# Two cross-attention layers on one core: another order of the loads and of every engine, energies of both halves together, the MLP in three groups

## The chip, the cores and the metric

One core of one Trainium2 chip runs the whole program. Times are microseconds (us) on the device, from the start of the execution to its end. "Before" is the kernel as it was, "after" the changed one.

## The reference

`x` and `ctx` (called `y` in the first layer) are 16 x 64 x 256. Layer 0 works on each of the 16 batches with channels in rows:

```python
x_q = einsum('oc,bcn->bno', w_qk, y);  x_k = einsum('oc,bcn->bon', w_qk, x)
x_v = einsum('oc,bcn->bon', w_v, x) + b_v
energy = einsum('bnc,bcm->bnm', x_q, x_k)             # 256 x 256 for each batch
attention = softmax(energy);  attention /= 1e-07 + attention.sum(axis=1, keepdims=True)
x_r = einsum('bcn,bnm->bcm', x_v, attention)
x = x + relu(einsum('oc,bcn->bon', w_t, x - x_r) + b_t)
```

Layer 1 is a transformer block on 64 tokens a batch, width 256:

```python
q = layer_norm(x) @ q_w + q_b;  k = ctx @ k_w + k_b;  v = ctx @ v_w + v_b      # 16 heads of 16
hidden = softmax(where(mask, q @ k.T * 0.25, min)) @ v @ cproj_w + cproj_b + x
out = hidden + gelu(layer_norm(hidden) @ fc_w + fc_b) @ proj_w + proj_b        # inner width 1024
```

## The kernel before

Two batches share the 128 partitions, so there are eight pairs, n = 0 to 7. Index e (0 or 1) is a batch of the pair: partitions 0 to 63 or 64 to 127. All tensors stay on chip; every engine has one long list of steps written out by hand, and runs it strictly in that order, with semaphore waits between engines. All eight PSUM banks are assigned by hand.

Layer 0, for each pair: `proj(n)` multiplies the pair by `gram` (w_qk times itself, into `gx`) and by the folded value weight (into `uext`); `energy(n, e)` makes one batch's 256 x 256 energies out of `ys` and `gx` with 64 rows of the array; `energy_max` (VectorE), `energy_exp` (ScalarE), `rowsum_inv` (VectorE) and `scale_u` (GpSimd) follow for each batch; `mix(n)` multiplies; `colsum_inv`, `mix_normed`, `relu_in`, `relu`, `residual` finish the pair. `wtx(n)` is w_t times x. An fp32 matmul is two MATMUL records in the trace.

The setup before the first pair: `wt`, `wv`, `wqk` are loaded; `wt` is turned, `gram` made, the two bias rows (`vec0_rows`) turned, and `wtv`, `wtbv` made. SyncE, ScalarE and GpSimd each issue some loads. Twelve records of `ones` times `ones` run ahead of all this.

Layer 1: `turn_ctx`, `make_keys`, `make_values`, `make_queries` run for two halves of four pairs. `scores(n)`, softmax steps on VectorE, ScalarE and GpSimd (`probs_normed`), `turn_probs`, `heads`, `cproj`, `hidden`, `hidden_norm`, `turn_hidden`, `hidden_weight`, `hidden_high`, `hidden_low` follow for each pair; the last three leave the normed activations as a high and a low part (`hidT`). The MLP runs for halves of four pairs: `fc(k)`, k = 0 to 15, makes 128 of the 1024 inner rows for 512 columns (three products of high and low parts, twice: six MATMULs); `gelu(k)` and `split_ff(k)` bring them to `ff`; `project(n)` is 24 MATMULs of 256 columns over the eight blocks of a half, and `result(n)` adds the residual before the output's DMA. `fc(8)` to `fc(15)` are the second half; their columns lie in the same `ff` as the first half's, so they are written only when `project(3)` is done.

## Time and profile before

| | us |
|---|---|
| median of 3 runs (lowest, highest) | 157.91 (156.69, 158.32) |
| the profiled execution, its own time | 157.12 |
| its span in the trace | 155.3 |
| TensorE busy | 144.1 (93%) |
| VectorE busy | 110.4 (71%) |
| ScalarE busy | 97.1 (63%) |
| GpSimd busy | 92.0 (59%) |

The span goes from the first to the last instruction in the trace; 1.8 us of the execution's time lie around it. Busy is the time in which an engine had at least one instruction under way, with the pipeline's fill and drain, so that an engine that is busy all the time need not be at its fastest; the distance from one start to the next tells what an instruction really takes of TensorE.

### The profile page before, as it was taken

To read this page: it belongs to the slowest core of one execution; us is meant where nothing else is said; L and a number is where in the kernel's file an instruction comes from. 1 tells how busy PE (TensorE), PEld (TensorE's weight loads), DVE (VectorE), ACT (ScalarE), POOL (GpSimd) and SP (SyncE) were. 2 spreads that over 40 slices of the span, in tenths; PEclk is the share of its full clock that TensorE was granted. 3 is DMA by queue.
4 is the path that set the end of the run, shared out by engine and by line. 5 is a ranking of instruction groups with operands and counts; after the bars stand their busy time and mean duration, and the time that the engine had idled before them with its cause. 6 is when DMAs were issued, how large, how long until landed. Compare 5 with 4: busy or idle time off the path is not lost.

```text
span 155.3 us, 3653 instructions
## 1 busy us (share of the span) xinstructions
PE 144.1 (93%) x1284; PEld 114.3 (74%) x1284; DVE 110.4 (71%) x249; ACT 97.1 (63%) x242; POOL 92.0 (59%) x148
## 2 busy tenths in 40 slices
PE   7369999999999989969999999999999999999993
PEld 6256767867778738836757686877788999789992
DVE  2232759999998769899798996999898120788211
ACT  2101668858698995898898999896971452453000
POOL 8950541696858787558879897559799372000000
PEclk9955999999999999999999999999999999999999
DMA  1999020002200020201010000000000110001011
GB/s 26 327 294 305 23 68 0 6 2 68 70 0 4 0 68 0 74 2 54 25 61 4 4 0 0 4 2 0 4 0 4 34 36 0 0 4 68 34 51 51
DMA packets 6787, 6.89 MB, mean 44 GB/s; under 512 B 1044, under 2 KB 6194, under 8 KB 6770
## 3 DMA queue, kind: packets, MB, share of 16 engines
q1 hardware_dynamic: 5808, 5.85, 11.7%
q10 hardware_dynamic: 674, 0.56, 1.2%
q0 software_dynamic: 288, 0.27, 0.7%
q8 instruction: 10, 0.16, 0.4%
q14 instruction: 7, 0.06, 0.1%
HBM read 5.62 MB, written 1.05 MB: 43 GB/s over the span
## 4 chain that ended last, share of the span: by engine, by line
PE 52%; ACT 16%; POOL 11%; issue 7%; DVE 5%; ACTq 0%; DVEq 0%; POOLq 0%
PE psum L754 48%; POOL probs L344 4%; POOL rows L349 2%; ACT vals L413 2%; ACT probs L463 2%; ACT hdT L383 2%; DVE smax L642 2%; ACT hn L480 2%; ACT keys L383 2%; ACT ys L499 1%; POOL hid_rstd_t L291 1%; POOL hidT_lo L354 1%; PE psum L880 1%; ACT att L427 1%; POOL rows L339 1%
## 5 line engine op out<-in xcount | busy, mean ns | idle before, releaser
L344 POOL TENSOR_TENSOR probs<-probs,pinv 128x512 f32<-128x512 f32 x16 | 18.1, 1139 | 6.2 <-DVE pinv L666 6.1
L319 POOL TENSOR_SCALAR us<-uext,rinv 128x128 f32<-128x128 f32 x32 | 12.6, 406 | 15.0 <-DVE rinv L614 14.8
L427 ACT ACTIVATE att<-psum,nmax 128x256 f32<-128x256 f32 x32 | 14.8, 473 | 7.9 <-DVE nmax L608 7.9
L754 PE MATMUL psum<-wpj_hi,ff_hi 128*128 128x256 f32 x64 | 18.4, 288 | 0.0
L754 PE MATMUL psum<-wpj_lo,ff_hi 128*128 128x256 f32 x64 | 18.0, 281 | 0.0
L754 PE MATMUL psum<-wpj_hi,ff_lo 128*128 128x256 f32 x64 | 17.9, 280 | 0.0
L499 ACT ACTIVATE ys<-psum,vec 128x512 f32<-128x512 f32 x16 | 11.0, 693 | 10.0 <-PE psum L754 8.0
L704 DVE CAST ff_hi<-ys 128x512 fp32r<-128x512 f32 x16 | 9.1, 569 | 8.8 <-ACT ys L499 8.8
L754 PE MATMUL psum<-att,us 128*128 128x256 f32 x64 | 15.2, 381 | 0.0
L754 PE MATMUL psum<-gx,ys 64*128 64x256 f32 x64 | 13.7, 434 | 0.4 <-issue 0.4
L608 DVE TENSOR_REDUCE nmax<-psum 128x2 f32<-128x512 f32 x16 | 10.7, 682 | 4.6 <-PE psum L754 4.4
L706 DVE TENSOR_TENSOR ff_lo<-ys,ff_hi 128x512 fp32r<-128x512 f32 x16 | 13.4, 839 | 0.5
L754 PE MATMUL psum<-hidT_hi,wfc_hi 128*128 128x512 f32 x32 | 13.1, 409 | 0.0
L754 PEld LDWEIGHTS psum<-att,us 128*128 128x128 f32 x64 | 11.6, 190 | 1.6 <-issue 0.3
L754 PE MATMUL psum<-hidT_lo,wfc_hi 128*128 128x512 f32 x32 | 12.7, 395 | 0.0
L754 PE MATMUL psum<-hidT_hi,wfc_lo 128*128 128x512 f32 x32 | 12.6, 395 | 0.0
L754 PEld LDWEIGHTS psum<-wpj_hi,ff_hi 128*128 128x128 f32 x64 | 12.1, 188 | 0.3 <-DVE ff_lo L706 0.2
L754 PEld LDWEIGHTS psum<-wpj_lo,ff_hi 128*128 128x128 f32 x64 | 12.1, 189 | 0.0
L754 PEld LDWEIGHTS psum<-wpj_hi,ff_lo 128*128 128x128 f32 x64 | 12.1, 188 | 0.0
L754 PEld LDWEIGHTS psum<-gx,ys 64*128 64x128 f32 x64 | 8.4, 202 | 4.1 <-ACT att L427 1.7
L661 DVE TENSOR_REDUCE psums<-probs 128x8 f32<-128x512 f32 x16 | 10.5, 669 | 0.5 <-ACT probs L463 0.3
L651 DVE TENSOR_TENSOR probs<-psum,smax 128x512 f32<-128x512 f32 x16 | 10.6, 681 | 0.2
(126 smaller groups left out, 382.8 us busy)
## 6 DMA issues: line engine op xcount, KB each, us to landing
wstage<-in_L_xattn_fc_w_dram SPq DMA_DIRECT2D x4, 256.0 KB, 4.9
wstage<-in_L_xattn_proj_w_dram SPq DMA_DIRECT2D x4, 256.0 KB, 2.7
out_dram<-rows SPq DMA_DIRECT2D x8, 128.0 KB, 1.7
ys<-in_ctx_dram SPq DMA_DIRECT2D x1, 512.0 KB, 6.1
rows<-in_x_dram SPq DMA_DIRECT2D x1, 512.0 KB, 7.3
ys<-in_ctx_dram ACTq DMA_DIRECT2D x1, 384.0 KB, 6.0
rows<-in_x_dram SPq DMA_DIRECT2D x1, 384.0 KB, 6.4
wk<-in_L_xattn_k_w_dram SPq DMA_DIRECT2D x1, 256.0 KB, 6.6
```

Source lines behind the costliest of these rows:

```text
L319: pool.tensor_scalar(us[:, n % 2, e, j, :], uext[:, n % 2, j, e * C:e * C + P], rinv[:, n % 2, e, j:j + 1], 1.0, ALU.mult, ALU.mult).then_ ...
L344: pool.tensor_tensor(half, half, pinv[:, n % 2, HEAD_HALVES[i]].unsqueeze(2).broadcast_to([P, H // 2, C]), ALU.mult).then_inc(S["probs_rea ...
L349: pool.tensor_tensor(rows[:, n, :], rows[:, n, :], proj_b[:], ALU.add).then_inc(S["hid_plus_bias"], 1)
L383: act.activation(dst, src, ACT.Identity, bias=bias, scale=scale).then_inc(S[done], 1)
L427: act.activation(att[:, n % 2, e, j, :], halfbank(ENERGY + e, j), ACT.Exp, bias=nmax[:, n % 2, e, j:j + 1], accum_out=rsum[:, n % 2, e, j: ...
L499: act.activation(act_ff[:, k % 2, :], bank(FC_BANK[k]), ACT.Gelu_apprx_tanh, bias=col(FC_B + k % M)).then_inc(S["gelu_ready"], 1)
L608: dve.tensor_reduce(nmax[:, n % 2, e, :], bank(ENERGY + e).rearrange("p (j m) -> p j m", j=2), AX.X, ALU.max, negate=True).then_inc(S["ene ...
L651: dve.tensor_tensor(probs[:, n % 2, i * BANK:(i + 1) * BANK].rearrange("p (j i k) -> p j i k", j=2, k=C), scores_ps[:, 2 * i:2 * i + 2].re ...
L661: dve.tensor_reduce(psums[:, n % 2, HEAD_HALVES[i]], half, AX.X, ALU.add).then_inc(S["probs_sum"], 1)
L704: dve.tensor_copy(ff[0][:, m, :], act_ff[:, k % 2, :]).then_inc(S["ff_hi"], 1)
L706: dve.tensor_tensor(ff[1][:, m, :], act_ff[:, k % 2, :], ff[0][:, m, :].bitcast(F32), ALU.subtract).then_inc(S["ff_lo"], 1)
L754: return pe.matmul(dst, lhsT, rhs, start=start, stop=stop)
```

## The change

- **Loads.** SyncE issues `w_qk` first (it was on ScalarE), then `w_t`, `w_v`, the two rows `b_v`, `b_t` (they were on GpSimd), then pairs 1 to 3 of `x`, the key and value weights, the second half of `ctx` and `x`, and only then the eight vectors of layer 1. ScalarE issues pair 0 of `x`, then pair 0 of `ctx`. The four small mask loads go from GpSimd to SyncE behind `q_w`.
- **Setup.** TensorE makes `gram` first; `proj(0)` is cut into `make_gx(0)`, ahead of `wtv` and the turned biases, and `make_u(0)`, behind the first energies. The energies of pair 0 come ahead of `wtbv`, of the turned context and of `proj`'s second part.
- **Energies.** `energy(n)` makes both batches of a pair in one step, one instruction of e = 0, one of e = 1 in turn, and waits until all four exponentials of pair n - 1 are done. In the kernel before both halves are steps of their own; between those of pairs 1, 5 and 6 other steps stand.
- **MLP.** `GROUPS` has three groups: pairs 0 to 3 (512 columns), 4 and 5 (256), 6 and 7 (256): 24 `fc` steps in place of 16, the last 16 half as wide. Group 1 writes columns 0 and 1 of `ff`, which pairs 0 and 1 had (`pairs_before` gives 2), group 2 columns 2 and 3 (it waits for four `project`).
- **Order.** All engines' lists are written anew, and the banks with them. Some waits that another one implies are left out.

```diff
-        CTX_BANK, KEYS_BANK = [4, 7, 5, 7], [7, 6, 4, 4]
-        VALUES_BANK, QUERIES_BANK = [6, 7, 5, 4], [0, 7, 7, 5]
-        FC_BANK = [5, 1, 0, 7, 3, 0, 4, 5, 6, 4, 6, 0, 1, 5, 0, 6]
-        PROJECT_BANK = [0, 5, 3, 2, 7, 3, 1, 5]
+        GROUPS = [(0, 4, 0), (4, 2, 0), (6, 2, 2)]
+        CTX_BANK, KEYS_BANK = [4, 6, 6, 7], [7, 7, 4, 7]
+        VALUES_BANK, QUERIES_BANK = [7, 5, 4, 5], [6, 7, 4, 5]
+        FC_BANK = [1, 0, 6, 2, 3, 0, 5, 2, 3, 0, 3, 0, 2, 5, 5, 3, 6, 4, 3, 6, 0, 4, 0, 3]
+        PROJECT_BANK = [7, 5, 1, 1, 7, 6, 0, 1]
+
+        def group_of(n):
+            return next((k, g) for k, g in enumerate(GROUPS) if g[0] <= n < g[0] + g[1])
+
+        def pairs_before(k):
+
+            at, end = GROUPS[k][2], GROUPS[k][2] + GROUPS[k][1]
+            return max([f + min(n, end - a) for f, n, a in GROUPS[:k] if a < end and at < a + n], default=0)
...
         def _(sp):
+            load_twice(sp, "w_qk", wqk, wqk_loaded)
             load_twice(sp, "w_t", wt0, wt_loaded)
             load_twice(sp, "w_v", wv0, wv0_loaded)
-            load_pairs(sp, "x", rows, x_loaded, 0)
+            load_vec(sp, 0, "b_v", L0_BV, vec0_loaded)
+            load_vec(sp, 0, "b_t", L0_BT, vec0_loaded)
             load_pairs(sp, "x", rows, x_loaded, 1)
             load_weight(sp, "k_w", wk, "k")
+            load_weight(sp, "v_w", wv, "v")
+            load_pairs(sp, "ctx_2048", ys, y_loaded, 2)
+            load_pairs(sp, "x", rows, x_loaded, 2)
             for name, at in (("ln1_w", LN1_W), ("ln1_b", LN1_B), ("q_b", Q_B), ("k_b", K_B), ("v_b", V_B),
                              ("ln2_w", LN2_W), ("ln2_b", LN2_B), ("fc_b", FC_B)):
                 load_vec(sp, 1, name, at, vec_loaded)
-            load_weight(sp, "v_w", wv, "v")
-            load_pairs(sp, "ctx_2048", ys, y_loaded, 2)
-            load_pairs(sp, "x", rows, x_loaded, 2)
             load_weight(sp, "q_w", wq, "q")
+            sp.wait_ge(mask_zeroed, 1)
+            for j in range(J):
+                sp.dma_start(mask8[32 * j:32 * j + 2, :, :], A["mask_BxS2_bf1"].rearrange(
+                    "(n e) k -> e n k", e=2)).then_inc(w_loaded["mask"], 16)
             load_weight(sp, "cproj_w", wc, "c")
...
-            load_vec(pool, 0, "b_v", L0_BV, vec0_loaded)
-            load_vec(pool, 0, "b_t", L0_BT, vec0_loaded)
+            pool.memset(uext[:], 1.0).then_inc(zeros_ready, 1)
             pool.memset(half_power[:], -0.5).then_inc(zeros_ready, 1)
-            pool.memset(uext[:], 1.0).then_inc(zeros_ready, 1)
+            pool.memset(mask8[:], 0).then_inc(mask_zeroed, 1)
             pool.memset(vals[:], 0.0).then_inc(zeros_ready, 1)
-            pool.memset(mask8[:], 0).then_inc(mask_zeroed, 1)
+            pool.wait_ge(zeros_ready, 3)
             pool.wait_ge(mask_zeroed, 1)
-            for j in range(J):
-                pool.dma_start(mask8[32 * j:32 * j + 2, :, :], A["mask_BxS2_bf1"].rearrange(
-                    "(n e) k -> e n k", e=2)).then_inc(w_loaded["mask"], 16)
-            pool.wait_ge(zeros_ready, 3)
...
-            load_twice(act, "w_qk", wqk, wqk_loaded)
+            load_pairs(act, "x", rows, x_loaded, 0)
             load_pairs(act, "ctx_2048", ys, y_loaded, 0)
             load_pairs(act, "ctx_2048", ys, y_loaded, 1)
...
-                wait(act, "mixed", 2 * (n - 2) + e + 1)
+                if e == 0:
+                    wait(act, "mixed", 2 * (n - 1))
...
-                act.activation(act_ff[:, k % 2, :], bank(FC_BANK[k]), ACT.Gelu_apprx_tanh,
+                width = GROUPS[k // M][1] * P
+                act.activation(act_ff[:, k % 2, 0:width], psum[:, FC_BANK[k], 0:width], ACT.Gelu_apprx_tanh,
                                bias=col(FC_B + k % M)).then_inc(S["gelu_ready"], 1)
...
-                m = k % M
+                m, (first, count, at) = k % M, GROUPS[k // M]
+                cols, src = slice(at * P, (at + count) * P), act_ff[:, k % 2, 0:count * P]
                 wait(dve, "gelu_ready", k + 1)
 
-                wait(dve, "mlp_made", NH * (k // M))
-                dve.tensor_copy(ff[0][:, m, :], act_ff[:, k % 2, :]).then_inc(S["ff_hi"], 1)
+                if m == 0:
+                    wait(dve, "mlp_made", pairs_before(k // M))
+                dve.tensor_copy(ff[0][:, m, cols], src).then_inc(S["ff_hi"], 1)
                 wait(dve, "ff_hi", k + 1)
-                dve.tensor_tensor(ff[1][:, m, :], act_ff[:, k % 2, :], ff[0][:, m, :].bitcast(F32),
+                dve.tensor_tensor(ff[1][:, m, cols], src, ff[0][:, m, cols].bitcast(F32),
...
+            def make_gx(n):
                 if n == 0:
                     pe.wait_ge(gram_ready, 2)
+                landed(pe, x_loaded, n)
+                mm(halfbank(PROJ0, 0), gram[:], rows[:, n, :]).then_inc(S["gx_made"], 1)
+
+            def make_u(n):
+                if n == 0:
                     pe.wait_ge(wtv_ready, 2)
-                landed(pe, x_loaded, n)
-                mm(halfbank(PROJ0, 0), gram[:], rows[:, n, :])
                 for j in range(2):
                     ins = mm(psum[:, PROJ0, D + j * P:D + (j + 1) * P], rows[:, n, j * P:(j + 1) * P], wtvT[:])
-                ins.then_inc(S["proj_made"], 1)
-
-            def energy(n, e):
+                ins.then_inc(S["u_made"], 1)
+
+            def proj(n):
+                make_gx(n)
+                make_u(n)
+
+            def energy(n):
                 wait(pe, "gx_ready", n + 1)
                 landed(pe, y_loaded, n)
-                r = slice(e * C, (e + 1) * C)
                 for j in range(2):
-                    ins = mm(halfbank(ENERGY + e, j), ys[r, n, j * P:(j + 1) * P], gx[r, n % 2, :])
-                ins.then_inc(S["energy_made"], 1)
+                    for e in range(2):
+                        r = slice(e * C, (e + 1) * C)
+                        ins = mm(halfbank(ENERGY + e, j), ys[r, n, j * P:(j + 1) * P], gx[r, n % 2, :])
+                        if j == 1:
+                            ins.then_inc(S["energy_made"], 1)
...
-                h, i = k // M, k % M
-                wait(pe, "hid_lo", NH * (h + 1))
+                (first, count, _), i = GROUPS[k // M], k % M
+                wait(pe, "hid_lo", first + count)
                 if k == 0:
                     wait(pe, "part_lo", WPARTS // 2)
                 for c in range(G):
                     for a, b in ((0, 0), (0, 1), (1, 0)):
-                        ins = mm(bank(FC_BANK[k]), wfc[a][:, c, i * P:(i + 1) * P],
-                                 hidT[b][:, c, h * TOK:(h + 1) * TOK], c == 0 and a + b == 0,
+                        ins = mm(psum[:, FC_BANK[k], 0:count * P], wfc[a][:, c, i * P:(i + 1) * P],
+                                 hidT[b][:, c, first * P:(first + count) * P], c == 0 and a + b == 0,
                                  c == G - 1 and (a, b) == (1, 0))
                 ins.then_inc(S["fc_made"], 1)
 
             def project(n):
-                h, i = n // NH, n % NH
+                k, (first, count, at) = group_of(n)
+                cols = slice((at + n - first) * P, (at + n - first + 1) * P)
                 if n == 0:
                     wait(pe, "part_lo", WPARTS)
                 for m in range(M):
-                    if i == 0:
-                        wait(pe, "ff_lo", M * h + m + 1)
+                    if n == first:
+                        wait(pe, "ff_lo", M * k + m + 1)
                     for a, b in ((0, 0), (0, 1), (1, 0)):
-                        ins = mm(halfbank(PROJECT_BANK[n], 0), ff[a][:, m, i * P:(i + 1) * P], wpj[b][:, m, :],
+                        ins = mm(halfbank(PROJECT_BANK[n], 0), ff[a][:, m, cols], wpj[b][:, m, :],
...
-            proj(0); pe.wait_ge(wtbv_ready, 1); turn_ctx(0, 0); energy(0, 0); energy(0, 1)
-            wait(pe, "u_ready", 1); proj(1); turn_ctx(0, 1); wtx(0); wait(pe, "energy_exp", 2); energy(1, 0)
...
+            keep_warm(6); make_gram(); turn_wt(); make_gx(0); make_wtv(); turn_vec0(); energy(0)
+            pe.wait_ge(bv_ready, 1); make_wtbv(); wait(pe, "gx_ready", 1); make_u(0); pe.wait_ge(gram_ready, 2)
+            wtx(0); pe.wait_ge(wtbv_ready, 1); turn_ctx(0, 0); wait(pe, "u_ready", 1); proj(1)
...
+            hidden_weight(6); hidden_high(6); hidden_normed(7); gelu(12); gelu(13); gelu(14); hidden_weight(7)
...
+            split_ff(5); split_ff(6); split_ff(7); hidden(6); hidden_mean_var(6); split_ff(8); split_ff(9)
+            result(0); result(1); split_ff(10); hidden(7); hidden_mean_var(7); split_ff(11); split_ff(12)
...
+            wait(pe, "gelu_ready", 5); fc(8); wait(pe, "gelu_ready", 7); turn_probs(7, 1); fc(9)
+            wait(pe, "hidf_ready", 12); project(0); wait(pe, "hidden_ready", 7); heads(7)
             wait(pe, "probst_ready", 16); project(1); wait(pe, "heads_ready", 16); cproj(7)
...
+            turn_hidden(7); wait(pe, "gelu_ready", 14); fc(14); fc(15); wait(pe, "out_ready", 3); project(3)
+            wait(pe, "hidden_ready", 8); fc(16); fc(17); wait(pe, "gelu_ready", 16); fc(18)
```

What TensorE is given between its warm-up and the energies of pair 0, before:

```order
L754 MATMUL psum<-ones 128x128 x6
L754 MATMUL psum<-ident,wt 64x64 x2
L754 MATMUL psum<-wqk 64x64 x2
L771 MATMUL psum<-ident,vec_rows 128x2
L754 MATMUL psum<-wtT,wv 64x64 x2
L754 MATMUL psum<-wtT,bv_cols 128x128
L754 MATMUL psum<-rows,gram 128x256
L754 MATMUL psum<-wtvT,rows 128x128 x2
L827 MATMUL psum<-ident,ys 128x128 x4
L754 MATMUL psum<-gx,ys 128x256 x4
L754 MATMUL psum<-rows,gram 128x256
```

And after, from `ones` to the first energies and behind them:

```order
L777 MATMUL psum<-ones 128x128 x6
L777 MATMUL psum<-wqk 64x64 x2
L777 MATMUL psum<-ident,wt 64x64 x2
L777 MATMUL psum<-rows,gram 128x256
L777 MATMUL psum<-wtT,wv 64x64 x2
L807 MATMUL psum<-ident,vec_rows 128x2
L777 MATMUL psum<-gx,ys 128x256 x4
L777 MATMUL psum<-wtT,bv_cols 128x128
L777 MATMUL psum<-wtvT,rows 128x128 x2
L777 MATMUL psum<-rows,wtT 128x256
L868 MATMUL psum<-ident,ys 128x128 x4
```

`gram` (`psum<-wqk`) and the `gx` product (`psum<-rows,gram`) now come early, the first energies (`psum<-gx,ys`) are the seventh row and not the tenth, and the turned context (`psum<-ident,ys`) stands behind them.

TensorE around the energies of pair 5, before:

```order
L754 MATMUL psum<-att,us 128x256 x4
L754 MATMUL psum<-gx,ys 128x256 x2
L754 MATMUL psum<-rows,wtT 128x256
L754 MATMUL psum<-gx,ys 128x256 x2
L754 MATMUL psum<-rows,gram 128x256
L754 MATMUL psum<-wtvT,rows 128x128 x2
L754 MATMUL psum<-att,us 128x256 x4
```

After:

```order
L777 MATMUL psum<-att,us 128x256 x4
L777 MATMUL psum<-gx,ys 128x256 x4
L860 MATMUL psum<-ident,xn 128x128 x2
L777 MATMUL psum<-rows,gram 128x256
L777 MATMUL psum<-wtvT,rows 128x128 x2
L777 MATMUL psum<-rows,wtT 128x256
```

The two halves of `psum<-gx,ys`, x2 each with `psum<-rows,wtT` between, have become one step x4.

ScalarE in the last third, from pair 7's turned probabilities on (`ys<-psum,vec` is a GELU), before:

```order
L499 ACTIVATE ys<-psum,vec 128x512 x2
L383 ACTIVATE hidf<-psum,vec 128x128 x2
L469 COPY prT<-psum 128x512 x2
L480 ACTIVATE hn<-rows,shift,hid_rstd_t 128x256
L383 ACTIVATE hdT<-psum,vec 128x128 x2
L493 CAST hidT_hi<-hidf 128x2x128
L383 ACTIVATE hidf<-psum,vec 128x128 x2
L493 CAST hidT_hi<-hidf 128x2x128
L480 ACTIVATE hn<-rows,shift,hid_rstd_t 128x256
L383 ACTIVATE hidf<-psum,vec 128x128 x2
L493 CAST hidT_hi<-hidf 128x2x128
L499 ACTIVATE ys<-psum,vec 128x512 x8
```

After:

```order
L483 COPY prT<-psum 128x512
L513 ACTIVATE ys<-psum,vec 128x256
L393 ACTIVATE hdT<-psum,vec 128x128 x2
L494 ACTIVATE hn<-rows,shift,hid_rstd_t 128x256
L513 ACTIVATE ys<-psum,vec 128x256 x2
L393 ACTIVATE hidf<-psum,vec 128x128 x2
L506 CAST hidT_hi<-hidf 128x2x128
L494 ACTIVATE hn<-rows,shift,hid_rstd_t 128x256
L513 ACTIVATE ys<-psum,vec 128x256 x3
L393 ACTIVATE hidf<-psum,vec 128x128 x2
L506 CAST hidT_hi<-hidf 128x2x128
L513 ACTIVATE ys<-psum,vec 128x256 x9
```

The eight GELUs of 512 columns in the last row before are sixteen of 256 columns, seven of which now stand between the steps of pairs 6 and 7.

## Rows read from the trace of the kernel before

**Rows 1.** The page of the profile: span, and busy time of each engine.

```profile
span 155.3 us, 3653 instructions
...
PE 144.1 (93%) x1284; PEld 114.3 (74%) x1284; DVE 110.4 (71%) x249; ACT 97.1 (63%) x242; POOL 92.0 (59%) x148
```

**Rows 2.** Windows: length, busy us (instructions) of PE, PEld, DVE, ACT, POOL; clock, DMA share, GB/s.

```profile
21.86:46.70 24.84, 24.46 (x126) 18.55 (x126) 23.41 (x60) 19.20 (x65) 16.09 (x32) 1.00 0.07 23
46.70:98.00 51.30, 48.26 (x662) 34.91 (x665) 44.93 (x101) 45.96 (x108) 40.88 (x62) 1.00 0.07 23
98.00:152.75 54.75, 54.54 (x432) 48.18 (x424) 32.83 (x61) 26.11 (x53) 22.60 (x31) 1.00 0.05 18
```

**Rows 3.** TensorE by time, 0 to 17 us: start, duration, operation, idle before.

```profile
1.05 2.93 PE L754 MATMUL psum<-ones 128*128 128x128 f32 x12 [1.05 <-POOL ones L268]
4.03 0.48 PE L754 MATMUL psum<-ident,wt 64*64 64x64 f32 x4
5.03 0.33 PE L754 MATMUL psum<-wqk 64*64 64x64 f32 x4 [0.52 <-DMA wqk<-in_L_xattn_w_qk_dram]
7.15 0.22 PE L771 MATMUL psum<-ident,vec_rows 2*128 2x2 f32 x1 [1.79 <-DMA vec_rows<-in_L_xattn_b_t_dram]
...
8.53 0.80 PE L754 MATMUL psum<-wtT,bv_cols 128*128 128x128 f32 x2 [0.90 <-DVE bv_cols L557]
...
12.79 2.09 PE L754 MATMUL psum<-gx,ys 64*128 64x256 f32 x8
...
16.75 1.13 PE L754 MATMUL psum<-gx,ys 64*128 64x256 f32 x4
```

**Rows 4.** Issue of the first loads: SyncE's first, and ScalarE's first and next.

```profile
0.80 0.66 SPq L224 DMA_DIRECT2D wt<-in_L_xattn_w_t_dram  x1
...
0.79 1.38 ACTq L224 DMA_DIRECT2D wqk<-in_L_xattn_w_qk_dram  x1
2.21 0.85 ACTq L231 DMA_DIRECT2D ys<-in_ctx_dram  x2
```

**Rows 5.** DMA issues by tensor: count, size, us from issue to landing.

```profile
rows<-in_x_dram SPq DMA_DIRECT2D x1, 128.0 KB, 4.8
ys<-in_ctx_dram ACTq DMA_DIRECT2D x1, 128.0 KB, 4.3
...
vec_rows<-in_L_xattn_b_t_dram POOLq DMA_DIRECT2D x1, 0.5 KB, 4.9
```

**Rows 6.** TensorE and its granted clock in single microseconds of the start (windows).

```profile
8.00:9.00 1.00, 0.47 (x2) 0.50 1.08 339
14.00:15.00 1.00, 1.00 (x7) 0.59 0.85 277
```

**Rows 7.** TensorE in order of time, the energies and what follows them.

```profile
21.86 1.14 PE L754 MATMUL psum<-gx,ys 64*128 64x256 f32 x8
...
25.73 1.14 PE L754 MATMUL psum<-gx,ys 64*128 64x256 f32 x8
26.80 0.70 PE L754 MATMUL psum<-rows,wtT 128*128 128x256 f32 x2
...
34.94 1.10 PE L754 MATMUL psum<-gx,ys 64*128 64x256 f32 x4 [0.37 <-issue]
35.97 0.70 PE L754 MATMUL psum<-rows,wtT 128*128 128x256 f32 x2
```

**Rows 8.** TensorE in order of time, one `fc` and one `project`, two starts of each.

```profile
102.43 0.39 PE L754 MATMUL psum<-hidT_lo,wfc_hi 128*128 128x512 f32 x1
102.67 0.40 PE L754 MATMUL psum<-hidT_hi,wfc_lo 128*128 128x512 f32 x1
...
117.00 0.28 PE L754 MATMUL psum<-wpj_hi,ff_hi 128*128 128x256 f32 x1
117.12 0.28 PE L754 MATMUL psum<-wpj_lo,ff_hi 128*128 128x256 f32 x1
```

**Rows 9.** Costliest groups on the page: ScalarE's exponentials.

```profile
L427 ACT ACTIVATE att<-psum,nmax 128x256 f32<-128x256 f32 x32 | 14.8, 473 | 7.9 <-DVE nmax L608 7.9
```

353 lines of the change are left out of this document (178 added, 175 removed).

## Prediction

> **What bounds the kernel now.** I read the page first: TensorE is busy for 144.1 of 155.3 us, no other engine for more than 110.4 [rows 1]. That is an average, so I asked for the same by stretch. From 21.86 to 46.70 TensorE is busy 24.46 of 24.84 us, from 46.70 to 98 us 48.26 of 51.30, and from there to the last matmul 54.54 of 54.75 [rows 2]. The reader should see two things there: the whole MLP part has 0.2 us of TensorE's time to give, and what TensorE waits for lies in the middle stretch (3.0 us) and ahead of 12.79 us. VectorE (44.93 of 51.30) and ScalarE (45.96) are close behind it in the middle stretch, so TensorE is the bound, but not by much.
>
> Busy need not be useful, so the third view is TensorE's list in order of time. At the start there are holes: 0.52 us for the load of `wqk`, 1.79 us for the turned bias row, 0.90 us for `bv_cols`; the first energies start only at 12.79 us, and run at half clock (x8 takes 2.09 us; later 1.14) [rows 3, 7]. The granted clock is 0.50 from 8 us on and is back at 1 within the microsecond from 14 us (0.59 in its mean): 1.2 and 2.4 GHz [rows 6]. It fell behind the hole of 1.79 us and rose after some six microseconds of nearly unbroken work.
>
> **Part 1, the start.** What leaves the path: the wait for `wqk` behind ScalarE's slow first issue (1.38 us against 0.66 us of SyncE's first, whose data the turning of `wt` found in place at 4.03) [rows 3, 4]; the bias rows' landing as a condition for everything; and `wtbv`, the second part of `proj(0)` and the turned context, which move behind the first energies.
>
> When can `energy(0)` start? `ys` of pair 0 keeps its place on ScalarE: issued at 2.21, 4.3 us to landing, 6.5 us [rows 4, 5]. `rows` of pair 0 becomes ScalarE's first load: 0.79 plus 4.8 gives 5.6; its product with `gram` at half clock takes two records, about 0.9, and a hop through VectorE another 0.9, which is what such a hop costs at 8.53: `gx` is there at 7.4 [rows 3 to 5]. The row `b_t` is SyncE's fifth load and its turning stands ahead of the energies in TensorE's list: 0.80 plus four issues of at most 0.66 is 3.4, plus 4.3 to 4.9 gives 7.7 to 8.3 [rows 4, 5]; it has half a kilobyte, so it may well be earlier. I take 7.8, 5.0 us ahead of today's 12.79.
>
> Not all of it is kept, since the moved steps are now between `energy(0)` and `energy(1)`. Today that distance is 16.75 - 12.79 = 3.96. The stretch from 8.53 to 12.79 (4.26 us) less the `gx` product (0.9) and a wait of some 0.7 leaves 2.7 us of steps that join it, at half clock. With today's clocks `energy(1)` would come at 7.8 + 3.96 + 2.7 = 14.5. At full clock throughout it is 7.8 + (3.96 - 1.0) + 1.35 = 12.1; at half clock throughout the 1.95 us now run after 14.8 double, 16.4. The holes of 1.79 and 0.90 shrink, so an earlier rise is likelier than a later one. I take 13.8, a gain of **3.0** (bounds 0.3 and 4.6). From there on TensorE has no idle time up to 46.7 to speak of, so a shift is kept.
>
> The other moved issues: the four mask loads now stand on SyncE ahead of `cproj_w` and the MLP weights, about four times 0.3 to 0.66, one to three microseconds later for loads that are used from some 33 us on; and SyncE's wait for the mask's memset, behind which `cproj_w` and the staged weights queue, ends long before SyncE comes to it at some 8 us, since GpSimd has only two small memsets ahead. GpSimd loses six issues before 12 us, where it waits anyway. I price all this at nothing; without that cover a late MLP weight would cost its delay once, up to 2 us.
>
> **Part 2, energies of both halves together.** The list shows x8 with 1.07 us from its start to the next step (25.73 to 26.80), and x4, one half alone, with 1.03 (34.94 to 35.97) [rows 7]. So the two halves, which use different 64 rows of the array, already run beside each other where they stand next to each other, and a half alone costs as much as both. Pairs 1, 5 and 6 have separate halves today, the other five stand together (pair 7 with a few ns between). The change therefore saves 3 x 1.03 = **3.1** us of TensorE, and nothing in the other pairs; turning e = 0 and e = 1 within a step changes nothing that the rows show.
>
> A rule of the Trainium skill speaks otherwise: "TensorE: Matmul & The Clock Gate", "The mechanism", says that matmuls start and end strictly in program order, and only weight loads are pulled ahead. By that rule x8 in today's order (four records of one half, then four of the other) would take twice an x4; the trace disagrees, with 1.14 us against 1.10.
>
> What it adds is a wait: `energy(n)` needs all four exponentials of pair n - 1, where the first half needed two. Queued behind it on TensorE are `proj(n+1)`, `wtx` and `mix(n-1)`, and VectorE's maxima wait for it. From pair 2 to pair 3 the halves stood together and the distance was 25.73 - 21.86 = 3.87 us without idle time [rows 7]; the mean distance of the five pairs from 21.86 to 46.70 is 24.84 / 5 = 4.97. Less two lone halves it is 4.55, above 3.87, so the new wait should mostly be over when it is reached.
>
> **Part 3, other engines.** With three microseconds less of TensorE's time, VectorE's 23.41 us and ScalarE's 19.20 [rows 2] have to fit in some 22.5 in the first stretch. VectorE's busy time holds overlapping tails, so this is no hard bound, yet some of the 3.1 will return as waits: I take **0.8** back (0 to 3.1). In the stretch from 46.7 to 98 us the order is new and I can't price it step by step: today's waits are 3.0 us in all, so it can't give more than that, and an equal loss bounds it above. I take 0: the engines' sums stay as they are, and the list is no denser.
>
> **Part 4, the MLP.** Two starts of an `fc` of 512 columns are 0.24 us apart (102.43, 102.67), of 256 columns 0.12 (117.00, 117.12) [rows 8]. The 48 records of `fc(8)` to `fc(15)` at 0.24 become 96 at 0.12; by the mean over a longer run of them (0.233, 0.118) that is 11.2 against 11.3 us, a cost of **0.1**. The gain can't be more than the 0.2 us that TensorE is idle from 98 us on. ScalarE gets eight GELUs more and VectorE eight more splits, under a stretch in which they are busy for 26.11 and 32.83 of 54.75 [rows 2]; at up to 1 us each they still fit. The shared columns add waits: `split_ff(8)` waits for `project(1)`, and `hidden(7)` is queued behind it, behind `split_ff(10)` and two results. I count some 4 us of VectorE there, then some 3 us of norm and turning, against `fc(10)` to `fc(13)` and `project(2)` on TensorE, 48 records of 0.118 or 5.7 us, and `cproj(7)`: about level, so between 0 and 1.5 us. I take 0.
>
> **The sum.** -3.0 - 3.1 + 0.8 + 0.1 = -5.2 us. The profiled execution took 157.12, so it would be 151.9. The median of the runs is 157.91, 0.8 above it; I forecast against the median: **152.7**. A difference of 1% (1.6 us) is about what this kernel's runs can tell from none.
>
> **The rivals.**
> - *The clock stays low to the end of the start.* The half-clock bound of part 1: gain 0.3 in place of 3.0, the rest as above, -2.5, 155.4 us. For it: the clock did fall there. Against: the hole before the fall shrinks. (The same page of the Trainium skill, "What's actually happening", calls the low clock the idle default; this trace agrees, with 0.50 behind the 1.79 us hole.) 15%.
> - *ScalarE or VectorE takes over.* All of the 3.1 comes back, and the middle stretch loses as much as it waits today, 3.0: -3.0 + 3.0 + 0.1, 158.0 us. For it: 90% and 88% busy in the middle. 12%.
> - *Slower: the loop over the exponentials.* ScalarE works 19.20 / 5 = 3.84 us a pair, of which four exponentials of 0.473 are 1.9 [rows 2, 9]. If none of the other 1.9 lay in the shadow of energies and maxima, since the order puts a `norm_weight` between the two halves of pair 6, the distance would be 3.87 + 1.9 = 5.8 and not 4.97: six times 0.83 is +5.0; with the start's -3.0 and 0.9, +2.9 or 160.8 us. It is slower by 1% from a distance of 5.6 on. 5%.
> - *More than forecast.* The full-clock start (4.6), nothing given back, and two of the three microseconds of waits in the middle gone: -9.6, 148.3 us; half of the surplus gives 150.5. 9%.
> - *The interleaving itself makes the overlap*, in all eight pairs: five more times 1.03, -10.4 and 147.5 us. That is the page's rule; [rows 7] speaks against it. 2%.
> - *The forecast*, 150.8 to 154.8: 57%.
>
> **Range and chances.** From 149.6 to 156.6: it takes in the low-clock case and part of the better one. Faster by over 1%: 57 + 15 + 9 + 2 = 83%; within 1%: 12%; slower: 5%.
>
> **What would show it.** First energies at 7.8 us and the second x8 at 13.8; eight energies of x8 with 1.07 us to the next step, none of x4; a distance of 4.5 us a pair; the clock's level from 8 to 14 us; TensorE's idle time in the middle near 3 us; `fc` of 256 columns at 0.118 from start to start and an end part without idle time. I am wrong if the energies' distance stays at 5, if the start's gain is gone by pair 2, or if TensorE waits ahead of `fc(14)` to `fc(18)`.

## The result, and the profile after

| | before | after |
|---|---|---|
| median of the runs | 158.12 us (4 runs, 156.69 to 158.86) | 152.04 us (4 runs, 151.90 to 152.48) |
| ratio | | 0.963 (95%: 0.956 to 0.970) |
| the profiled execution | 157.12 us, span 155.3 | 152.17 us, span 150.4 |

Faster by 3.7%; the forecast was 152.7. A few executions of a kernel run over 1.5% longer than its fastest: here and below they count in the medians and the highest times, and not in the ratios. The page of the kernel after, span and busy time of each engine, against [rows 1]:

```profile
span 150.4 us, 3717 instructions
...
PE 140.8 (94%) x1332; PEld 114.6 (76%) x1332; DVE 116.2 (77%) x265; ACT 99.3 (66%) x250; POOL 87.2 (58%) x142
```

TensorE lost 3.3 us of busy time. VectorE shows 5.8 us more, although its work grew only by eight splits: 4 us of that is one cast in the start, shown below. Windows of after, the three stretches that answer to [rows 2] (from the x8 of pair 2 to that of pair 7, to the first `fc`, to the end):

```profile
18.72:42.76 24.04, 23.79 (x133) 18.46 (x132) 23.00 (x61) 20.31 (x67) 17.32 (x34) 1.00 0.08 26
42.76:96.00 53.24, 50.41 (x698) 36.78 (x698) 48.36 (x106) 48.28 (x114) 41.88 (x67) 1.00 0.08 22
96.00:150.40 54.40, 51.03 (x427) 47.32 (x426) 32.56 (x71) 25.39 (x54) 19.71 (x26) 1.00 0.06 21
```

TensorE's gap in the middle is 2.8 us, against 3.0 before. (In the last row 3.4 us are not busy: the row runs to the end of the span, 2.6 us past the last matmul, and holds two waits of 0.4 us each, shown under e9.) The start, TensorE in order of time, against [rows 3]:

```profile
1.05 2.93 PE L777 MATMUL psum<-ones 128*128 128x128 f32 x12 [1.05 <-POOL ones L282]
4.37 0.48 PE L777 MATMUL psum<-wqk 64*64 64x64 f32 x4 [0.39 <-DMA wqk<-in_L_xattn_w_qk_dram]
6.42 0.48 PE L777 MATMUL psum<-ident,wt 64*64 64x64 f32 x4 [1.58 <-DMA wt<-in_L_xattn_w_t_dram]
6.83 1.22 PE L777 MATMUL psum<-rows,gram 128*128 128x256 f32 x2
...
8.58 2.08 PE L777 MATMUL psum<-gx,ys 64*128 64x256 f32 x8
10.59 0.79 PE L777 MATMUL psum<-wtT,bv_cols 128*128 128x128 f32 x2
...
14.86 1.14 PE L777 MATMUL psum<-gx,ys 64*128 64x256 f32 x8
```

`energy(0)` starts at 8.58 in place of 12.79 and `energy(1)` at 14.86 in place of 16.75. The reader should see a hole that wasn't there: 1.58 us for `wt`, which had been in place at 4.03. Its half-clock length (2.08 for x8) is unchanged.

The energies further on, against [rows 7]:

```profile
31.31 1.14 PE L777 MATMUL psum<-gx,ys 64*128 64x256 f32 x8
32.37 0.44 PE L860 MATMUL psum<-ident,xn 128*128 128x128 f32 x2
...
36.43 1.13 PE L777 MATMUL psum<-gx,ys 64*128 64x256 f32 x8
37.49 0.70 PE L777 MATMUL psum<-rows,wtT 128*128 128x256 f32 x2
```

From start to next step it is 1.06 us, in pairs 5 and 6 too.

**One ruler for all runs.** Three marks on TensorE cut every trace: the start of `energy(1)`, the start of `energy(7)`, and the last record of `project(7)`. Each number is a difference of two starts in the TensorE list, in us, taken in ns and then rounded, so that it may be 0.01 off the rows; before it is 152.43 - 16.75, after 147.57 - 14.86:

| kernel | energy(1) at | to energy(7) | to the last record | both | median of runs |
|---|---|---|---|---|---|
| before | 16.75 | 29.68 | 106.00 | 135.68 | 158.1 |
| after | 14.86 | 27.90 | 104.82 | 132.72 | 152.04 |
| e1_adjacent | 17.71 | 28.85 | 105.94 | 134.79 | 156.89 |
| e2_not_turned | 14.87 | 27.93 | 104.78 | 132.71 | 151.95 |
| e3_apart | 13.92 | 31.12 | 104.25 | 135.37 | 154.46 |
| e4_old_loads | 14.74 | 27.92 | 104.77 | 132.69 | 152.95 |
| e5_old_setup | 18.87 | 27.90 | 104.81 | 132.71 | 155.67 |
| e6_two_halves | 15.65 | 27.90 | 104.44 | 132.34 | 152.23 |
| e7_warm | 12.59 | 27.90 | 104.79 | 132.70 | 150.47 |
| e8_clean_start | 12.69 | 27.90 | 104.81 | 132.71 | 150.05 |
| e9_tail | 15.26 | 27.91 | 103.96 | 131.87 | 151.59 |
| e10_all | 11.60 | 27.91 | 103.97 | 131.88 | 148.55 |
| e11_cast_late | 14.56 | 27.91 | 104.80 | 132.71 | 151.77 |
| e12_best | 13.59 | 27.90 | 104.06 | 131.96 | 148.49 |

Seven kernels that have the same work and order behind `energy(1)` (after, e2, e4, e5, e7, e8, e11) agree in "both" within 0.03 us, while their `energy(1)` is spread over six microseconds. What differs among these seven profiles is the start, and whatever is won there is kept whole. So I read each profile by the ruler. If the part behind `energy(1)` is the same in all runs of a kernel (only one run of each has a trace), a median less the "both" of its row says how a typical start goes: 22.4 us before, 19.3 after.

### The profile page after: what moved, and what is told of

It is laid out like the page before. It is cut to its first block, busy times and chain, and to the rows that moved or that the text cites. A ratio compares the mean times of both kernels' runs of the same rounds, so it can differ in the third digit from the quotient of the medians.

```text
span 150.4 us, 3717 instructions
## 1 busy us (share of the span) xinstructions
PE 140.8 (94%) x1332; PEld 114.6 (76%) x1332; DVE 116.2 (77%) x265; ACT 99.3 (66%) x250; POOL 87.2 (58%) x142
## 3 DMA queue, kind: packets, MB, share of 16 engines
HBM read 5.62 MB, written 1.05 MB: 44 GB/s over the span
## 4 chain that ended last, share of the span: by engine, by line
PE 39%; POOL 20%; issue 17%; DVE 17%; DMA 3%; ACT 2%; SPq 0%; POOLq 0%; DVEq 0%; ACTq 0%
PE psum L777 37%; POOL probs L354 5%; DMA wt<-in_L_xattn_w_t_dram 3%; POOL rows L359 2%; POOL hid_rstd_t L300 2%; DVE nmax L628 2%; POOL hidT_lo L364 2%; DVE probs L670 2%; POOL wpj_lo L321 2%; DVE xn L655 2%; ACT vals L424 1%; POOL us L329 1%; DVE mixn L640 1%; POOL shift L310 1%; PE psum L921 1%
## 5 line engine op out<-in xcount | busy, mean ns | idle before, releaser
L439 ACT ACTIVATE att<-psum,nmax 128x256 f32<-128x256 f32 x32 | 14.8, 474 | 11.6 <-DVE nmax L628 11.6
L513 ACT ACTIVATE ys<-psum,vec 128x256 f32<-128x256 f32 (+1 forms) x24 | 12.9, 545 | 14.3 <-PE psum L777 10.9
L725 DVE CAST ff_hi<-ys 128x256 fp32r<-128x256 f32 (+1 forms) x24 | 10.0, 415 | 12.7 <-ACT ys L513 8.6
L329 POOL TENSOR_SCALAR us<-uext,rinv 128x128 f32<-128x128 f32 x32 | 11.8, 383 | 13.7 <-DVE rinv L633 13.3
L727 DVE TENSOR_TENSOR ff_lo<-ys,ff_hi 128x256 fp32r<-128x256 f32 (+1 forms) x24 | 15.9, 661 | 0.8
L777 PE MATMUL psum<-hidT_hi,wfc_hi 128*128 128x256 f32 (+1 forms) x48 | 16.1, 336 | 0.0
L777 PE MATMUL psum<-hidT_hi,wfc_lo 128*128 128x256 f32 (+1 forms) x48 | 15.3, 318 | 0.0
L777 PE MATMUL psum<-hidT_lo,wfc_hi 128*128 128x256 f32 (+1 forms) x48 | 15.3, 318 | 0.0
L777 PEld LDWEIGHTS psum<-wpj_hi,ff_hi 128*128 128x128 f32 x64 | 12.1, 188 | 0.7 <-DVE rows L733 0.6
L777 PEld LDWEIGHTS psum<-wpj_hi,ff_lo 128*128 128x128 f32 x64 | 12.1, 188 | 0.0
L777 PEld LDWEIGHTS psum<-wpj_lo,ff_hi 128*128 128x128 f32 x64 | 12.1, 188 | 0.0
L921 PE MATMUL psum<-ident,probs 128*128 128x128 f32 x64 | 9.9, 280 | 1.3 <-POOL probs L354 0.6
L476 ACT ACTIVATE probs<-probs 128x512 f32<-128x512 f32 x16 | 9.6, 626 | 2.2 <-DVE probs L670 2.2
L660 DVE TENSOR_REDUCE smax<-psum 128x16 f32<-128x1024 f32 x8 | 9.7, 1209 | 1.3 <-PE psum L777 1.3
```

What stands on the lines that cost most here:

```text
L329: pool.tensor_scalar(us[:, n % 2, e, j, :], uext[:, n % 2, j, e * C:e * C + P], rinv[:, n % 2, e, j:j + 1], 1.0, ALU.mult, ALU.mult).then_ ...
L439: act.activation(att[:, n % 2, e, j, :], halfbank(ENERGY + e, j), ACT.Exp, bias=nmax[:, n % 2, e, j:j + 1], accum_out=rsum[:, n % 2, e, j: ...
L476: act.activation(half, half, ACT.Exp, scale=SCALE).then_inc(S["probs_exp"], 1)
L513: act.activation(act_ff[:, k % 2, 0:width], psum[:, FC_BANK[k], 0:width], ACT.Gelu_apprx_tanh, bias=col(FC_B + k % M)).then_inc(S["gelu_re ...
L660: dve.tensor_reduce(smax[:].rearrange("p (j i) -> p j i", j=J), scores_ps.rearrange("p j (i k) -> p j i k", k=C), AX.X, ALU.max).then_inc( ...
L725: dve.tensor_copy(ff[0][:, m, cols], src).then_inc(S["ff_hi"], 1)
```

## The experiments

**e1_adjacent**, the kernel before with the halves of pairs 1, 5 and 6 side by side (pair 5 shown, the others likewise):

```
-            energy(5, 0); wait(pe, "relu_in", 3); wtx(3); wait(pe, "energy_exp", 20); energy(5, 1)
+            energy(5, 0); wait(pe, "energy_exp", 20); energy(5, 1); wait(pe, "relu_in", 3); wtx(3)
```

> The kernel before, with one edit: in pairs 1, 5 and 6 the second half's energies stand right behind the first half's on TensorE, as in the other five pairs; the steps between them (the products of the next pair, a turning, a wtx) come behind. The energies are written e = 0, then e = 1, not alternating. My theory (the two halves of 64 rows run beside each other where their records are neighbours, however they are ordered): three lone x4 of 1.03 us vanish, all eight pairs show x8 with about 1.07 us to the next step, and the time falls by 3.1 us, up to 0.8 of it given back as waits: -2.3 to -3.1. Rival, other engines set the loop's rate (VectorE and ScalarE near their limit, the exponentials now waited for): less than 1 us. Rival, only the alternation makes the halves overlap: 0.

Measured: 156.89 us (10 runs), ratio 0.993 (0.990 to 0.997), so -1.1; the ruler gives -0.89. A miss for my number. TensorE in order of time shows where it went:

```profile
35.10 1.80 PE L754 MATMUL psum<-gx,ys 64*128 64x256 f32 x8 [0.28 <-issue]
36.83 0.70 PE L754 MATMUL psum<-rows,wtT 128*128 128x256 f32 x2
...
40.42 0.44 PE L819 MATMUL psum<-ident,xn 128*128 128x128 f32 x2 [0.29 <-DVE xn L636]
40.86 1.22 PE L754 MATMUL psum<-gx,ys 64*128 64x256 f32 x8
```

The x8 of pair 5 is 1.80 us long: its second half waits for the exponentials of pair 4 and starts 0.67 behind the first, a wait which `wtx(3)` had covered. Pair 6 starts 5.76 us behind pair 5, against 5.79 in the kernel before. Only pair 1 gained (4.30 us to pair 2 in place of 5.11). Putting the halves together frees TensorE's time, but without a new order of the other engines' lists two thirds of it come back as waits.

**e2_not_turned**, the kernel after with the two loops of `energy` exchanged:

```
-                for j in range(2):
-                    for e in range(2):
+                for e in range(2):
+                    for j in range(2):
```

> The kernel after, with one edit: within energy(n) the loop over the halves is outside and the loop over the column blocks inside, as in the kernel before; nothing else stands between them. My theory (halves overlap as neighbours, in either order): no difference, within 0.5 us; x8 with 1.07 us to the next step in all pairs. Rival, the alternation is what makes the two halves overlap: each of the eight pairs costs 1.03 us more on TensorE, +6 to +8 us.

Measured: 151.95 us, and 132.71 on the ruler against 132.72. The alternation that the change writes out is worth nothing:

```profile
18.74 1.14 PE L777 MATMUL psum<-gx,ys 64*128 64x256 f32 x8
19.81 0.48 PE L777 MATMUL psum<-rows,gram 128*128 128x256 f32 x1
```

**e3_apart**, the kernel after with one step between the halves of pairs 1, 5 and 6 again (pair 5 shown):

```
+            def energy(n, halves=(0, 1)):
-            wait(pe, "energy_exp", 20); energy(5); wait(pe, "ctx_lo", 2); turn_x1(0)
+            wait(pe, "energy_exp", 20); energy(5, (0,)); wait(pe, "ctx_lo", 2); turn_x1(0); energy(5, (1,))
```

> The kernel after, with one edit: in pairs 1, 5 and 6 one step (proj(2), turn_x1(0), wtx(4)) stands between the energies of the first and of the second half, so these halves stand alone. My theory: three x4 of about 1.03 us more on TensorE, +3.1 us, less up to 0.8 that was given back as waits: +2.3 to +3.1. Rival, the loop is bound by ScalarE and VectorE once it is this dense: less than 1 us. Rival, the energies' share of the gain is small and the start's is large: also below 1.

Measured: 154.46 us, ratio to before 0.978 (0.971 to 0.985) against 0.963 of after, so +2.4; +2.65 on the ruler, of which +3.22 up to `energy(7)` and -0.57 behind it. Three of its rows:

```profile
37.48 1.13 PE L777 MATMUL psum<-gx,ys 64*128 64x256 f32 x4
38.53 0.70 PE L777 MATMUL psum<-rows,wtT 128*128 128x256 f32 x2
39.16 1.13 PE L777 MATMUL psum<-gx,ys 64*128 64x256 f32 x4
```

A half alone takes 1.05 us to the next step, three times 1.05 is 3.15. The rival, a loop bound by ScalarE and VectorE, falls for the kernel after: there they keep pace at 27.90. With e1 it says that the saving and the new order of the other lists belong together: 0.89 by the one without the other, 2.65 with both.

**e4_old_loads** and **e5_old_setup** make a square of the start. e4 gives the kernel after the issues and memsets of before:

```
         def _(act):
-            load_pairs(act, "x", rows, x_loaded, 0)
+            load_twice(act, "w_qk", wqk, wqk_loaded)
```

(and so on SyncE and GpSimd). e5 keeps the new loads and takes the old order of steps (TensorE's list shown; VectorE's and ScalarE's go back with it):

```
-            keep_warm(6); make_gram(); turn_wt(); make_gx(0); make_wtv(); turn_vec0(); energy(0)
-            pe.wait_ge(bv_ready, 1); make_wtbv(); wait(pe, "gx_ready", 1); make_u(0); pe.wait_ge(gram_ready, 2)
-            wtx(0); pe.wait_ge(wtbv_ready, 1); turn_ctx(0, 0); wait(pe, "u_ready", 1); proj(1)
+            keep_warm(6); turn_wt(); make_gram(); turn_vec0(); make_wtv(); make_wtbv(); proj(0)
+            pe.wait_ge(wtbv_ready, 1); turn_ctx(0, 0); energy(0); wait(pe, "u_ready", 1); proj(1)
```

> The kernel after, with the order of issues and memsets of the kernel before on SyncE, ScalarE and GpSimd; the engines' work is after's. What its trace showed of after: w_t landed only at 6.4 us beside ScalarE's x and ctx loads, and VectorE's cast of select took 4.29 us beside GpSimd's long memset; energy(0) came at 8.58. Theory A (the reordered setup steps on TensorE make the gain of the start, the loads hardly): w_t is back at 4.0, w_qk comes at about 4.5, x of pair 0 lands near 7, energy(0) at 8.5 to 9.5, and the time is that of after, 0 to +0.7. Rival B (the new order of loads makes the gain, above all the b_t row, which lands at 7.7 from GpSimd's queue): energy(0) again near 11 to 12.8 and +2 to +3 us. Rival C (the late w_t and the held VectorE cost after more than the new order brings): faster by 0.5 to 1.5.

> The kernel after with its own loads, but with the setup steps up to energy(0) in the order of the kernel before on TensorE, VectorE and ScalarE: turning of w_t, gram, bias row, wtv, wtbv, both parts of proj(0) and the turned context all ahead of energy(0). With the run of after on old loads this completes the square. Theory A (the order of the setup steps makes the gain of the start): energy(0) falls back to about 12, energy(1) to about 16, +1.5 to +3 us. Rival B (the loads make it): the bias row is here at 7 in place of 8.5, energy(0) at about 10 and energy(1) as in after, below +0.7.

Measured: e4 152.95 us (152.03 to 153.39), `energy(1)` at 14.74; its profiled execution was the fastest of the four, so the loads may be worth up to 0.9 in the others, a little more than the 0.7 I had allowed. e5 155.67 us, `energy(1)` at 18.87: +3.6, where I had expected 1.5 to 3, and `energy(0)` at 13.30. `energy(1)` of the square: old and old 16.75, old loads and new steps 14.74, new and new 14.86, new loads and old steps 18.87. The order of the steps makes the gain, 2.0 or 4.0 us.

What the new loads do by themselves these four profiles don't settle. Where `w_t` comes first they seem to cost 2.1 us, but only 0.5 of it is there at `energy(0)` (13.30 against 12.79); the other 1.6 is a longer low clock, since the steps behind it run at their long durations up to 18 us (1.22 us for the next pair's gx product, against 0.70 before). By medians less "both", the typical starts are 22.42 (old steps) and 20.26 (new steps) with the old loads, 22.96 and 19.32 with the new ones: 2.2 or 3.6 us for the order of the steps, and for the loads a cost of 0.5 with the old order and a gain of 0.9 with the new one.

e4's start waits elsewhere:

```profile
4.88 0.48 PE L776 MATMUL psum<-wqk 64*64 64x64 f32 x4 [0.91 <-DMA wqk<-in_L_xattn_w_qk_dram]
5.15 0.42 PE L776 MATMUL psum<-ident,wt 64*64 64x64 f32 x4
7.12 1.19 PE L776 MATMUL psum<-rows,gram 128*128 128x256 f32 x2 [1.54 <-DMA rows<-in_x_dram]
```

and e5's stands for `w_t` from the end of the ones on:

```profile
6.86 0.48 PE L777 MATMUL psum<-ident,wt 64*64 64x64 f32 x4 [2.88 <-DMA wt<-in_L_xattn_w_t_dram]
```

The hole has changed its owner: `x` with the old loads, `w_t` with the new, and the first energies come within 0.3 us of each other.

**e6_two_halves**, the kernel after with the MLP in two groups of four pairs and before's lists from `make_values(1, 1)` on:

```
-        GROUPS = [(0, 4, 0), (4, 2, 0), (6, 2, 2)]
+        GROUPS = [(0, 4, 0), (4, 4, 0)]
```

> The kernel after with the MLP in two groups of four pairs as in the kernel before, and with the order of the kernel before on all engines from make_values(1, 1) on; start, energies and middle are after's. My theory (three groups cost 0.1 in more starts, and gain nothing, since TensorE waits for nothing there): -0.5 to +0.5 us; the trace of after showed two waits of 0.6 and 0.5 us in its MLP part, so rather a gain. Rival (the smaller groups are what lets the MLP begin early and hides the last pairs' norms once the part ahead is faster): +1.5 us or more, as new waits ahead of the second group's fc.

Measured: 152.23 us, but its profiled execution had a late start (15.65); on the ruler 132.34, 0.38 better than after. The three groups, with the lists written for them, gain nothing.

**e7_warm**, more products of ones in the holes of TensorE's start:

```
-            keep_warm(6); make_gram(); turn_wt(); make_gx(0); make_wtv(); turn_vec0(); energy(0)
+            keep_warm(8); make_gram(); keep_warm(4); turn_wt(); make_gx(0); keep_warm(2); make_wtv()
+            turn_vec0(); energy(0)
```

> The kernel after with more products of ones on TensorE in the holes of the start: sixteen records in place of twelve at the beginning, eight behind gram, where it waits for w_t, and four behind the gx product. In after, energy(0) runs at half clock (x8 2.08 us) and full spacing comes only from 12.8 us on. Theory A (the clock rises after some four to six microseconds of unbroken work, whatever that is): the clock is full before energy(0), x8 takes about 1.07, energy(1) comes at 13 to 13.5 in place of 14.9, -1.3 to -1.9 us. Rival B (the steps between energy(0) and energy(1) wait for other engines and loads, so a higher clock gives little): below 0.5. Rival C (the clock's rise does not depend on it): 0, or +0.2 for the added records.

Measured: 150.47 us, ratio 0.952 (0.948 to 0.955), -1.6; `energy(1)` at 12.59 in place of 14.86.

```profile
1.05 3.64 PE L777 MATMUL psum<-ones 128*128 128x128 f32 x16 [1.05 <-POOL ones L282]
4.62 0.33 PE L777 MATMUL psum<-wqk 64*64 64x64 f32 x4
4.88 1.16 PE L777 MATMUL psum<-ones 128*128 128x128 f32 x8
6.51 0.33 PE L777 MATMUL psum<-ident,wt 64*64 64x64 f32 x4 [0.47 <-DMA wt<-in_L_xattn_w_t_dram]
...
8.26 1.13 PE L777 MATMUL psum<-gx,ys 64*128 64x256 f32 x8
```

`energy(1)` comes a little ahead of the 13 to 13.5 expected. The same x8 takes 1.13 us in place of 2.08, and its start is only 0.3 earlier: the gain is the 6.28 us from `energy(0)` to `energy(1)` that became 4.33. The clock is at the upper of its two levels (2.4 GHz) when gram starts, behind 3.6 us of unbroken records (gram takes 0.33 us, against 0.48 in after), and stays there; the longest hole is 0.47 us. The "four to six microseconds" of theory A are not borne out as a rule.

In the kernel after, with holes of 0.39 and 1.58 us, records have their full-clock spacing only from 12.8 on. Of the eleven profiles with twelve ones, before's included, ten have an x8 of 1.93 to 2.09 us for `energy(0)`; the eleventh is e8, below, with 1.57. In two of the ten, e3 and e6, the clock was up at the turning of `wt` (0.33) and fell again, and in the kernel before it was up at gram. So with twelve ones the clock at this point differs from profile to profile.

**e8_clean_start** and **e11_cast_late**. e11 moves VectorE's cast to `select`:

```
-            evict_gram(); evict_wt(); evict_gx(0); evict_vec0(); evict_wtv(); energy_max(0, 0); evict_wtbv()
+            evict_gram(); evict_wt(); evict_gx(0); evict_vec0(); evict_wtv(); select_rows(); energy_max(0, 0); evict_wtbv()
```

(`select_rows()` is the wait and the `tensor_copy` that stood at the top), and e8 moves a load as well:

```
         def _(sp):
             load_pairs(sp, "x", rows, x_loaded, 1)
+            load_pairs(sp, "ctx_2048", ys, y_loaded, 1)
         def _(act):
-            load_pairs(act, "ctx_2048", ys, y_loaded, 1)
```

> The kernel after with two edits of the start: VectorE's cast to select stands behind the eviction of wtv in place of first (in after it took 4.29 us beside GpSimd's memset of vals, where before it took 0.23), and the load of ctx for pairs 1 to 3 is issued by SyncE behind the x load in place of by ScalarE, so that w_t's small packets don't share the DMA engines with it. Theory A (the two costs of the new start are on its path): w_t in place by 5 us, energy(0) at about 7.5, energy(1) 0.6 to 1.2 earlier, as much off the time. Rival B (the path goes through other steps, above all wv's landing and x, and the half clock): within 0.4. Rival C (ctx of pair 1 now lands too late for the turned context): +0.5 or more.

> The kernel after with only one of the two edits of the run with the clean start: the cast to select stands behind the eviction of wtv; ScalarE still issues the load of ctx for pairs 1 to 3 at the start. It parts the 2.0 us that both gave. Theory A (w_t's landing at 6.4 us is what holds the path; the gram copies are over by then even behind the long cast): 0, within 0.4. Rival B (the held VectorE delays gx): -0.5 to -1.5.

Measured: e8 150.05 us (148.47 to 151.59), ratio 0.946 (0.940 to 0.953), -2.0, `energy(1)` at 12.69, more than the 0.6 to 1.2 expected; e11 151.77 us, 14.56. The cast is worth nothing by itself, though it is the strangest row of the kernel after. VectorE and GpSimd in order of time:

```profile
1.79 4.29 DVE L555 CAST select<-is_row 128x128 bf16<-128x128 f32 x1
4.97 1.39 DVE L561 COPY gram<-psum 64x64 f32<-64x64 f32 x2
6.94 0.48 DVE L561 COPY wtT<-psum 64x64 f32<-64x64 f32 x2 [0.58 <-PE psum L777]
...
2.49 3.51 POOL L289 MEMSET vals<- 128x4096 f32 x1
```

It ends at 6.08, with the memset's 6.00; in e8, where it runs later, it takes 0.23 us:

```profile
5.29 0.33 PE L779 MATMUL psum<-ident,wt 64*64 64x64 f32 x4 [0.67 <-DMA wt<-in_L_xattn_w_t_dram]
...
6.76 1.57 PE L779 MATMUL psum<-gx,ys 64*128 64x256 f32 x8
...
7.69 0.23 DVE L575 CAST select<-is_row 128x128 bf16<-128x128 f32 x1
```

"SBUF — State Buffer", "SBUF: two separate sides", in the Trainium skill, says that a VectorE operation in a two-port mode and a GpSimd operation share a pair of ports as an exclusive lock, held for a whole instruction. The trace agrees if this cast is such an operation, which no run here shows: it took 4.29 us beside the memsets and 0.23 without.

The load is the larger part of e8's gain, and not the whole. With 384 KB less beside it, the turning of `w_t` starts at 5.29 and not at 6.38 as in e11, 1.1 us earlier, but the first energies start 1.8 earlier. The other 0.7 is the clock: from the turning of `wt` to `energy(0)` it is 2.16 us in e11 and in after, 1.47 in e8, and 1.48 in e3, whose loads are after's and whose `w_t` is late:

```profile
6.51 0.33 PE L777 MATMUL psum<-ident,wt 64*64 64x64 f32 x4 [1.63 <-DMA wt<-in_L_xattn_w_t_dram]
...
7.99 1.93 PE L777 MATMUL psum<-gx,ys 64*128 64x256 f32 x8
```

So the load itself is worth 1.1 us: eight profiles with it in its old place turn `w_t` at 6.32 to 6.86. Whether the shorter hole also kept the clock up in e8, or chance did, one profile can't tell; the medians of e8 and e11 are 1.7 us apart. Without ScalarE's load and with the cast still early wasn't run; the gram copies would then end at 6.36 as in after, behind the turning of `wt` at 5.29.

**e9_tail** takes away the two waits that the MLP part of after shows:

```profile
103.81 0.63 PE L921 MATMUL psum<-ident,probs 128*128 128x128 f32 x4 [0.44 <-POOL probs L354]
...
127.80 0.39 PE L777 MATMUL psum<-wpj_hi,ff_hi 128*128 128x256 f32 x1 [0.39 <-DVE rows L733]
```

```
-        PROJECT_BANK = [7, 5, 1, 1, 7, 6, 0, 1]
+        PROJECT_BANK = [7, 5, 1, 2, 7, 6, 0, 1]
-            x1_plus_bias(7); hidden_plus_bias(4); hidden_norm(5); low_part(6); probs_normed(6, 1)
+            x1_plus_bias(7); hidden_plus_bias(4); hidden_norm(5); probs_normed(6, 1); low_part(6)
-            turn_hidden(7); wait(pe, "gelu_ready", 14); fc(14); fc(15); wait(pe, "out_ready", 3); project(3)
+            turn_hidden(7); wait(pe, "gelu_ready", 14); fc(14); fc(15); project(3)
```

> The kernel after with the two waits of its MLP part taken away: project(3) writes bank 2, which is free then, in place of bank 1, so it needs no result(2) first (that wait was 0.54 us); and on GpSimd probs_normed(6, 1) stands ahead of low_part(6), so that turn_probs(6, 1) needn't wait for it (0.60 us). Theory A (TensorE is the bound there, nothing else is late): -1.1 us, -0.5 at the least. Rival B (with these gone the next step waits for another engine, since the splits on VectorE and the memory passes on GpSimd are late as well): 0 to -0.3.

Measured: 151.59 us, -0.45 by the medians; 131.87 on the ruler, -0.85. By the starts of the records the two waits were 0.60 and 0.54 us (the idle time in the rows is counted from modelled ends); 0.29 of the 1.14 came back, and TensorE now waits some 0.5 us ahead of `turn_probs(7, 1)`.

**e10_all** puts e8, e9 and the ones (`keep_warm(8)`, behind gram `keep_warm(2)`, behind gx `keep_warm(1)`) together.

> The kernel after with the clean start (cast later, ctx of pairs 1 to 3 issued by SyncE), more products of ones in the holes (sixteen records, then four behind gram and two behind the gx product) and the two waits of the MLP part taken away. If the three are independent: energy(0) at 6.7, 1.07 us for it, 3.3 us of steps at full clock, energy(1) at 11.0 to 11.4 in place of 14.9; from energy(1) to the last projection the runs of after agree within 0.05 us, so the shift is kept: -3.5, and -0.5 to -1.1 for the MLP part: 147.3 to 148.0 us. Rival (the steps at full clock now run ahead of the loads: ctx of pair 1 or x of pair 1 lands at 9.5 to 10): energy(1) at 12, 148.5 or more.

Measured: 148.55 us (148.07 to 148.85), ratio 0.943 (0.939 to 0.947): faster than the kernel after, whose interval (0.956 to 0.970) lies apart. `energy(0)` at 7.17, `energy(1)` at 11.60, 131.88 behind it. The expected 147.3 to 148.0 is missed: by 0.07 in the profiled execution (148.07), the fastest of the six, and by 0.55 in the median, which lies where the rival was put, though `energy(1)` didn't come as late as the rival's 12. The sixteen ones hold gram until 4.74, where it had `w_qk` at 4.29 in e8, which is why `energy(0)` isn't at 6.7.

**e12_best** shortens them and moves one pass on GpSimd:

```
-            keep_warm(8); make_gram(); keep_warm(2); turn_wt(); make_gx(0); keep_warm(1); make_wtv()
+            keep_warm(7); make_gram(); keep_warm(2); turn_wt(); make_gx(0); keep_warm(1); make_wtv()
-            probs_normed(7, 0); hidden_low(4); low_part(7); hidden_low(5); hidden_plus_bias(5)
-            probs_normed(7, 1); hidden_norm(6); hidden_norm(7)
+            probs_normed(7, 0); hidden_low(4); low_part(7); hidden_low(5); probs_normed(7, 1)
+            hidden_plus_bias(5); hidden_norm(6); hidden_norm(7)
```

> The kernel of the run with all three edits, with two small mends that its trace asks for: fourteen records of ones at the beginning in place of sixteen (there they ended after w_qk had landed and held gram for 0.35 us), and on GpSimd probs_normed(7, 1) ahead of hidden_plus_bias(5), since TensorE waited 0.5 us for it at the second half of pair 7. If TensorE is the bound in both places: energy(1) 0.2 to 0.35 earlier and the distance from energy(1) to the last projection 131.4 in place of 131.9: 147.7 to 148.1 us. Rival (both are covered by something else): 148.5 as that run.

Measured: 148.49 us, spread from 147.86 to 152.05 over seven runs: no better than e10, and less steady. The profiled execution took 150.23 and kept the low clock to about 10 us:

```profile
1.05 3.35 PE L779 MATMUL psum<-ones 128*128 128x128 f32 x14 [1.05 <-POOL ones L283]
4.39 0.48 PE L779 MATMUL psum<-wqk 64*64 64x64 f32 x4
4.80 1.22 PE L779 MATMUL psum<-ones 128*128 128x128 f32 x4
...
8.54 1.85 PE L779 MATMUL psum<-gx,ys 64*128 64x256 f32 x8
...
109.86 0.66 PE L923 MATMUL psum<-ident,probs 128*128 128x128 f32 x4 [0.36 <-ACT ys L513]
```

The 0.35 us saved ahead of gram is there (4.39 for 4.74), and lost several times over by the clock. Why it stayed low isn't settled: the records stand nearly as close as in e10, and one profile can't tell fourteen ones from chance. The wait ahead of `turn_probs(7, 1)` has ScalarE's GELU as its releaser and not GpSimd: the rival holds, 131.96.

## Why the prediction was right, step by step

| term | forecast | measured | from |
|---|---|---|---|
| start | -3.0 (-0.3 to -4.6) | -1.9 | energy(1) 16.75 to 14.86 |
| lone halves, after waits | -3.1 + 0.8 | -2.65 | e3 against after |
| middle stretch, rest | 0 | -0.7 | remainder: -2.96 + 2.65 - 0.38 |
| MLP | +0.1 | +0.4 | e6 against after |
| sum | -5.2 | -4.9 | 157.12 to 152.17 |

These are the two profiled executions. The sum was met in part by luck: the start gave 1.1 less than forecast and what lies behind it 0.8 more. The medians fell by 6.1, from 158.12 to 152.04, since the profiled execution of before was 1.0 below its median and that of after 0.1 above. If the 2.96 us behind `energy(1)` hold in every run, the typical start gained 3.1, as forecast, and it is the profiled one of before that was early. No trace shows this.

**Part 1 had the mechanism right and the size off.** `energy(0)` was forecast for 7.8 and came at 8.58, `energy(1)` for 13.8 and came at 14.86. The step that failed is the one that took the turning of `wt` to be in place: "whose data the turning of `wt` found in place at 4.03". That held for SyncE's first load, issued ahead of all large ones. As its second, beside 640 KB that ScalarE had issued, `w_t` came at least 2.4 us later (0.7 of it by its issue), and its turning stands ahead of the gx product in TensorE's list. I priced the bias row as the last to come (7.7 to 8.3), and it was there in time: in e8 it is turned at 6.54. The `x` of pair 0, put at 5.6, came far earlier:

```profile
rows<-in_x_dram ACTq DMA_DIRECT2D x1, 128.0 KB, 2.1
```

Issued at 0.79 it landed at 2.9 and not after 4.8 us, so I had counted `x` 2.7 us too late and `w_t` 2.4 too early; that 7.8 comes within 0.8 of 8.58 is partly luck. The clock's part was sound as a range: the low clock lasted to 12.8, earlier than before's 14.8 and longer than I took, and e7 shows what the full one gives, `energy(1)` at 12.59 where the text had 12.1.

**Part 2 holds in its main points.** Eight x8, with 1.06 to 1.07 to the next step from pair 1 to pair 6; a lone half costs 1.05 (e3); the alternation nothing (e2). The rule of the Trainium skill that I set against the rows ("TensorE: Matmul & The Clock Gate", "The mechanism": matmuls start and end strictly in program order) would have made e2 slower by 6 to 8 us; it measured 0.0, and in its trace records of the two halves start in pairs 13 ns apart, so for records on different 64 rows of the array it doesn't hold as a bound on the time. The distance: (42.76 - 18.72) / 5 is 4.81. In it are two steps that stood behind `energy(7)` before, `make_keys(0, 0)` with 1.47 us (39.04 to 40.51) and `wtx(5)` with 0.53 (42.23 to 42.76); 4.41 a pair without them, forecast 4.5. The 4.97 of the text ends at 46.70, in the midst of pair 7; from first start to first start the kernel before has (46.43 - 21.86) / 5 = 4.91. What the text doesn't say and e1 shows: this saving needs the other lists' new order. It would have been 0.9 alone.

**Part 3**: 0.57 came back behind `energy(7)` for 0.8 forecast. In the middle I took no gain, and 0.7 was left; it is the remainder of the ledger, and no run isolates it. Little of it is in the overlap, which wasn't as full before as I took it ("a few ns between"): the second halves of pairs 4 and 7 start 0.13 and 0.24 us behind the first. Pair 4 in the kernel before:

```profile
30.11 1.22 PE L754 MATMUL psum<-gx,ys 64*128 64x256 f32 x8
```

The two pairs take 1.16 and 1.30 us to the next step, against 1.06 and 1.24 in the kernel after: 0.2 in all.

**Part 4**: two starts of an `fc` of 256 columns are 0.12 apart, as forecast:

```profile
126.55 0.28 PE L777 MATMUL psum<-hidT_hi,wfc_hi 128*128 128x256 f32 x1
126.67 0.28 PE L777 MATMUL psum<-hidT_lo,wfc_hi 128*128 128x256 f32 x1
```

But "an end part without idle time" is wrong by the two waits that e9 removes. I had looked for the stall at `split_ff(8)` and `hidden(7)` (0 to 1.5, taken as 0); there is none. It sits at `project(3)`, which shares bank 1 with `project(2)` and so waits for its result behind fourteen splits, and at `probs_normed(6, 1)`, behind a pass of 1.5 us. I read which data the steps share, and not which banks.

**The rivals.** The low clock was the nearest to come true: it lasted to 12.8, e7 prices it at 2.3 us against a start at full clock (1.6 by the medians), and with `w_t`'s wait it left 1.9 of the 3.0 and not 0.3. Both figures come from one profile each, and the clock differs between profiles of nearly the same start. The slower loop over the exponentials is what e1 shows in small, in the old order of lists.

## What to carry to other kernels

Cut every trace at the same two or three steps and compare the pieces: here it parted 0.03 us of noise from six microseconds of difference in the start, and gave prices that medians could not. Before a start is priced from one profile, hold it against the medians: by them the start gained 3.1 us, by the profiles 1.9. A saving on the bounding engine is as large as the other engines' lists allow (0.9 or 2.65 us for the same edit), so order them anew with it. When loads change places, price the landing of each small load beside the new neighbour on the other queue, and see that TensorE has unbroken work from the first microsecond on: ones in the holes gave 1.6 us (a start at full clock isn't guaranteed by them: e12).

## What the hardware showed that I had not expected

- A cast of 128 x 128 to bf16 on VectorE took 4.29 us beside GpSimd's memsets, the last of 2 MB, and 0.23 us without them.
- In both profiles with sixteen ones and filled holes the clock was full from gram on (x8 of `energy(0)` 1.13 and 1.14 us); in the one with fourteen it wasn't (1.85). In e8 it was full at gram and fell to 0.50 by 8 us, although TensorE had been busy for 0.96 of the microsecond from 6 and all of that from 7. The clock column of the windows says 1.00 over the whole start of after, where x8 takes 2.08: durations of equal records are the surer sign.

```profile
5.00:6.00 1.00, 0.71 (x6) 0.52 (x6) 0.53 (x3) 0.00 (x0) 1.00 (x1) 1.00 0.13 30
6.00:7.00 1.00, 0.96 (x9) 0.60 (x9) 0.72 (x4) 0.00 (x0) 0.00 (x0) 1.00 0.91 198
7.00:8.00 1.00, 1.00 (x8) 0.56 (x6) 0.86 (x4) 0.00 (x0) 0.00 (x0) 0.67 1.06 366
8.00:9.00 1.00, 1.00 (x5) 0.74 (x4) 0.65 (x1) 0.00 (x0) 0.00 (x0) 0.50 1.05 336
```

  (windows of e8 in single microseconds, columns as in [rows 2])
- A load of 32 KB landed 1.1 us later beside 384 KB more on another engine's queue (e11 against e8); moving those 384 KB behind it, with the cast out of the way, gave the kernel 2 us, of which the profiles put 0.7 down to the clock.
